# Split products of a compressed-interaction layer: which of their three matmul terms TensorE does on the first visit and which on the second

## The reference, cut to what matters

```python
def _cin(x, weights, biases):
    B, F, D = x.shape
    hidden = x
    finals = []
    for i, (w, b) in enumerate(zip(weights, biases)):
        size = w.shape[0]
        z = jnp.einsum('bhd,bfd->bhfd', hidden, x).reshape(B, hidden.shape[1] * F, D)
        y = jnp.einsum('bcd,oc->bod', z, w) + b[None, :, None]
        y = jax.nn.relu(y)
        if i != n_layers - 1:
            hidden, direct = (y[:, :size // 2, :], y[:, size // 2:, :])
        else:
            direct = y
        finals.append(direct)
    return jnp.concatenate(finals, axis=1).sum(-1)
```

## Time and profile before

| | us |
|---|---|
| median of 3 runs | 1091.94 (1091.52 to 1092.54) |
| the profiled execution, own time | 1092.62 |
| its span, first to last instruction | 1090.8 |
| TensorE busy | 1025.0 (94%) |
| VectorE busy | 944.4 (87%) |
| GpSimd busy | 915.5 (84%) |
| ScalarE busy | 734.9 (67%) |

### The profile page before, as it was taken

One profiled execution on the slowest core, in us unless ns is written; L12 is line 12 of the kernel. 1 busy time (PEld: TensorE's weight loads), 2 busy tenths in 40 slices (PEclk: granted clock), 3 DMA queues, 4 the chain that ended last, 5 costly groups with the idle time before them and its releaser, 6 DMA issues.

```text
span 1090.8 us, 10701 instructions
## 1 busy us (share of the span) xinstructions
PE 1025.0 (94%) x3493; PEld 651.4 (60%) x3493; DVE 944.4 (87%) x623; ACT 734.9 (67%) x907; POOL 915.5 (84%) x300
## 2 busy tenths in 40 slices
PE   2059999999999999999999999999999999999999
PEld 1025556656666666666666666666666666666664
DVE  4059999999999999999999999999998989888982
ACT  1036666767777677777777777777777777777761
POOL 7526878779999999999999899997989888988890
PEclk9569999999999999999999999999999999999999
DMA  4278777687878787778877878787777877786730
GB/s 137 55 188 200 194 186 184 180 198 190 210 178 205 183 213 187 192 191 199 207 185 192 201 181 208 182 206 194 194 184 194 204 183 187 191 208 184 183 84 1
DMA packets 142074, 196.89 MB, mean 180 GB/s; under 512 B 15858, under 2 KB 57458, under 8 KB 141891
## 3 DMA queue, kind: packets, MB, share of 16 engines
q1 hardware_dynamic: 137922, 192.01, 70.3%
q0 software_dynamic: 4096, 4.20, 1.8%
HBM read 175.18 MB, written 20.97 MB: 180 GB/s over the span
## 4 chain that ended last, share of the span: by engine, by line
PE 86%; DVE 4%; issue 4%; DMA 3%; ACT 2%; SPq 1%; DVEq 0%; ACTq 0%
PE py L610 40%; PE py L626 15%; PE py L616 14%; PE py L617 14%; DVE zf L498 2%; ACT zh L362 2%; PE py L631 1%; DMA xs<-x_dram 1%; DMA x_dram<-xf 1%; DMA xs<-in_L_rec_w 1%; PE pt L592 1%; DVE zl L515 1%; PE py L675 0%; PE pzS L675 0%; DVE zf L459 0%
## 5 line engine op out<-in xcount | busy, mean ns | idle before, releaser
L303 POOL TENSOR_TENSOR zl<-zf,zh 128x2048 fp32r<-128x2048 f32 x168 | 772.3, 4610 | 116.2 <-ACT zh L362 114.2
L498 DVE TENSOR_TENSOR zf<-xs,hid 128x2048 f32<-128x2048 f32 x256 | 583.3, 2283 | 67.1 <-ACT hid L377 51.9
L610 PE MATMUL py<-zf,wf 128*128 128x512 f32 x1072 | 485.2, 596 | 6.5 <-DVE zf L498 6.5
L362 ACT ACTIVATE zh<-zf 128x2048 fp32r<-128x2048 f32 x186 | 354.9, 1908 | 44.5 <-DVE zf L498 41.1
L610 PEld LDWEIGHTS py<-zf,wf 128*128 128x128 f32 x1072 | 203.5, 190 | 214.2 <-issue 194.2
L616 PE MATMUL py<-zh,wh 128*128 128x512 f32 x744 | 293.6, 395 | 8.7 <-ACT zh L362 8.7
L617 PE MATMUL py<-zh,wl 128*128 128x512 f32 x744 | 292.1, 393 | 0.0
L626 PE MATMUL py<-zl,wh 128*128 128x512 f32 x744 | 233.8, 436 | 0.0
L498 DVE TENSOR_TENSOR zf<-xs,px 128x2048 f32<-128x2048 f32 x64 | 146.4, 2288 | 37.8 <-DMA xs<-x_dram 35.9
L626 PEld LDWEIGHTS py<-zl,wh 128*128 128x128 f32 x744 | 135.9, 189 | 59.2 <-issue 29.2
L293 POOL DMA_INDIRECT emb<-in_tbl,idx x128 | 143.1, 1118 | 29.9 <-issue 24.5
(11 more groups left out here) (71 smaller groups left out, 439.8 us busy)
## 6 DMA issues: line engine op xcount, KB each, us to landing
xs<-x_dram SPq DMA_DIRECT2D x640, 256.0 KB
x_dram<-xf SPq DMA_DIRECT2D x64, 320.0 KB
emb<-in_tbl,idx POOLq DMA_INDIRECT x128
xs<-in_L_rec_w SPq DMA_DIRECT2D x2, 512.0 KB
xs<-in_L_rec_w SPq DMA_DIRECT2D x1, 1024.0 KB
wt<-in_W_top SPq DMA_DIRECT2D x1, 512.0 KB
wt1b<-in_W_top SPq DMA_DIRECT2D x1, 256.0 KB
wt1a<-in_W_top SPq DMA_DIRECT2D x1, 128.0 KB
```

The lines of the kernel that those rows point to most:

```text
L303: pool.tensor_tensor(zl[:, q], zf[:, s], zh[:, q].bitcast(F32), ALU.subtract).then_inc(lo["P"], 1)
L362: act.activation(zh[:, q], zf[:, s], ACT.Copy).then_inc(hi, 1)
L498: dve.tensor_tensor(zf[:, slot(u)], left, right, ALU.mult).then_inc(mult, 1)
L610: mm = pe.matmul(y, wf[:, w, h], zf[:, s, h], start=first and h == 0, stop=ends and h == T - 1)
```

## The change

Of a split unit's three terms, main now does wl x zh alone (4 matmuls) and late does the other two, wh x zl and wh x zh, in turn for each slab (8 matmuls). The order of the visits, the waits, the number of matmuls (12 for a unit) and everything on the other engines stay as they are. The "first" flag that clears the bank moves to wl x zh; the closing flag and the increment of used_split stay on the last matmul of late.

```diff
@@ -613,8 +613,7 @@
                     q, w = split_slot(u), SPLIT_NAMES.index(name)
                     pe.wait_ge(hi, NTH_SPLIT[u])
                     for h in range(T):
-                        pe.matmul(y, wh[:, w, h], zh[:, q, h], start=first and h == 0, stop=False)
-                        pe.matmul(y, wl[:, w, h], zh[:, q, h], start=False, stop=False)
+                        pe.matmul(y, wl[:, w, h], zh[:, q, h], start=first and h == 0, stop=False)
 
             def late(u):
                 name, g = u
@@ -623,7 +622,8 @@
                 q, w, y, ends = split_slot(u), SPLIT_NAMES.index(name), bank(u), closing(g) == u
                 need_low(pe, u)
                 for h in range(T):
-                    mm = pe.matmul(y, wh[:, w, h], zl[:, q, h], start=False, stop=ends and h == T - 1)
+                    pe.matmul(y, wh[:, w, h], zl[:, q, h], start=False, stop=False)
+                    mm = pe.matmul(y, wh[:, w, h], zh[:, q, h], start=False, stop=ends and h == T - 1)
                 mm.then_inc(used_split, 1)
```

## The result

The changed kernel takes 1111.6 us (median of five runs) against 1092.5 for the kernel before. The ratio of the two is 1.0165, 95% interval 1.0153 to 1.0178; of 1092.5 that makes 18.0 us (16.7 to 19.4), where the bare medians differ by 19.0. The kernel is slower, as forecast: 16.7 us and a time of 1108.6, in a range from 1099 to 1113, had been worked out.

What follows compares the result with a forecast made beforehand. TensorE, busy for 94% of the span, was taken to bound the kernel. Terms of 10.1 + 5.7 + 0.9 = 16.7 us on 1092.62 gave 1109.3, less 0.7 for the median 1108.6; range 1099 to 1113.

Steps and rivals of the forecast that it cites:

- The work is the same, only the moments move: Whole kernel: 744 matmuls of each term before and after; only the moments at which TensorE asks move.
- Part 1: Periods 0 to 10: each pair lasts 1.83 us longer; period 11 starts 11 steps of 0.915 us late, 10.1 us.
- Part 2: Periods 11 to 62: nine waits for D's product on VectorE at 0.62 us each, plus 0.1 us: 5.7 us.
- Periods 18 and 33: Two of eleven periods with low C on VectorE; older waits before A(19), A(34) absorb theirs: 0.1 us together.
- Late B: Periods 11 to 62: low part asked for a step earlier, B(26) tightest, 0.2 us short; nothing taken, 0.8 us if counted.
- the sign named against the prediction: Waits on zl appearing in the changed kernel would show the forecast wrong; no size given.
- Part 3: The end: closing late C(63) has 8 matmuls instead of 4 with nothing beside it: 0.9 us.
- A cheaper second load (1): In late, the pair's second load falls away, spacing 0.2145 us: 8 to 10.8 us less, 1098 to 1101; chance 0.08.
- a faster second matmul (2): In late, the second matmul follows at the load's 0.189 us: 30 us less, 1079; chance 0.03.
- Only the waits for D (3): Periods 0 to 10: if ScalarE absorbs the later turn_x, five steps go from the loss: 1104; chance 0.1.
- Nothing waits (4): Earlier needs are met because VectorE runs ahead once TensorE is late: 1092; chance 0.04.
- The clock (5): Odd periods' new 1.4 us waits drop TensorE to half clock; five falls of about 1.7 us give 1117; chance 0.05.

Runs made afterwards that it cites:

- e1: Changed kernel with main doing wh x zh and late wh x zl and wl x zh, same matmul numbers: 1111.3 us, ratio to kernel before 1.0174.
- e2: Kernel before with the change made for split units of periods 0 to 10 alone: 1103.5 us, ratio to kernel before 1.0102.
- e10: Changed kernel with turn_x ahead of main P in periods 1, 3, 5, 7 and 9 alone: 1100.8 us, ratio to kernel before 1.0066.
- e5: Kernel before with the change made for the C units alone: 1128.7 us, ratio to kernel before 1.0343.
- e3: Kernel before with the change made for split units of periods 11 to 42 alone: 1100.9 us, ratio to kernel before 1.0073.
- e4: Kernel before with the change made for split units of periods 43 to 63 alone: 1093.4 us, ratio to kernel before 1.0006.
- e9: Kernel before with the change made for the B units alone: 1111.4 us, ratio to kernel before 1.0164.
- e8: Kernel before with turn_x moved ahead of main P: 1087.5 us, ratio to kernel before 0.9956.

## Why the prediction was right, point by point

- **The work is the same, only the moments move.** Shown: equal counts, equal spacing, and e1 at the changed kernel's time.
- **Part 1, 10.1 us.** Shown. e2 gave 11.1 us for 11 steps and the boundary step, 11.0 expected; the loop's TensorE part grew by 1.84 us and its other part by 0.01; e10, which shortens only that loop, takes away 10.8 us. The waits before B that e5 shows have the same cause: high B stands behind xf in one queue.
- **Part 2, 5.7 us.** The mechanism held, the term was too small: the nine waits were priced at 0.62 us. From tail(12), the last before D(12), to tail(44) the changed kernel lost 18.1 - 11.1 = 7.0 us; e3 as a whole measured 8.0, with an interval of more than 2 us to either side. "0.30 us of slack" was the step that was off. In the traces TensorE never starts sooner than 0.05 us after the product's end, so only 0.25 of it was slack, and a unit that starts after a wait takes 3.70 us instead of 3.59, a cost of restart that rows 6 already had beside D(6) and that I had not counted: 0.915 - 0.25 + 0.11 = 0.78 us, times nine 7.0. Periods 18 and 33 were right: their waits were eaten by the older ones before A(19) and A(34), and they brought 0.1 us together.
- **Late B**, "I take nothing": wrong for two periods, and one reading was off. The tightest late B of the kernel before is not B(26) with 0.71 us but B(35) with 0.63; B(14) has 0.68 and B(20) 0.70. In the changed kernel two of them wait for their low part, B(20) and B(35). GpSimd's low B(20), then TensorE's late B(20):

```profile
418.25 4.65 POOL L303 TENSOR_TENSOR zl<-zf,zh 128x2048 fp32r<-128x2048 f32 x1
...
422.95 0.50 PE L625 MATMUL py<-zl,wh 128*128 128x512 f32 x1
```

  The low part ends at 422.90. The cover that the prediction counted on, the delay of TensorE from the V period before, was not there, as 18 and 33 had brought almost none. The tail starts move by 0.4 us at B(20) and by 0.5 at B(35), more than the 0.2 that the page counts as idle. It adds nothing to the sum: the D that follows, D(21) or D(36), then brings 0.4 or 0.3 us instead of 0.8. So the sign named against the prediction came; it touched the small terms only.
- **Part 3, 0.9 us.** From tail(60) to the end the difference goes from 18.1 to 19.0 us. e4's total cannot show it, since in it the first main A of the part is short as well and gives the same step back.
- **The sum** was 16.7 against 18.0 measured (16.7 to 19.4): 1.3 of it is part 2. The profiled execution itself stands 19.0 above the other, as it lost another 1 us at the start. The forecast time, 1108.6, is 3.0 below the measured one; besides part 2 and the difference between ratio and medians, the five runs of the kernel before had a median 0.6 us above that of the three it started from. By the prediction's own list the chances of slower are 0.93 and of faster 0.03, not 0.92 and 0.04.
- **Rivals.** A cheaper second load (1) and a faster second matmul (2): no, pairs are spaced like all others. Only the waits for D (3): no, it would leave 5 steps out, and e10 shows what the loop weighs. Nothing waits (4): no. The clock (5): no, it is 1.00 from 83 to 1100 us; the pauses of up to 1.4 us ahead of main B came and did not lower it. Before 83 us the two profiles do differ in clock, but not by the change (last section).

## What to carry to other kernels

When a hand-ordered engine is busy all the time, moving its work between two visits is not free though the sum stays: write down by how much each input is asked for sooner and each result handed on later, and set that against the slack read from the timeline. Do it for every wait of the engine and every loop through it: the two misses here (main A in e9, late B(20) and B(35)) were waits that had not been listed one by one. The sum over kinds of units is no guide (here A 0, B 18, C 37, all three 18 us); the loops are. A tiny instruction that another engine's queue stands behind, here a transpose ahead of xf and high B, deserves an earlier place before any of the large work is rearranged; here that alone made the kernel before 4.8 us faster.

## What the runs showed that was not expected

- A pause of TensorE costs more than its length: the eight f32 records of a whole unit that starts after one take 3.70 us from first start to last end instead of 3.59, and the first fp32r spacing is 0.31 us instead of 0.23, at a granted clock of 1.00.
- The start scatters between profiled executions, and in the two main profiles the difference is the clock. tail(1) stands between 0.8 us before (e1) and 2.5 us after (the changed kernel) that of the kernel before, in kernels that differ until then in A(0) or turn_x alone. Main P(1) and the window from 78 to 81 us (columns as rows 2) in the kernel before, then in the changed kernel:

```profile
77.82 3.60 PE L610 MATMUL py<-zf,wf 128*128 128x512 f32 x8
78.00:81.00 3.00, 3.00 (x9) 1.32 (x8) 2.94 (x3) 2.26 (x3) 2.55 (x3) 1.00 0.55 137
...
77.63 6.29 PE L610 MATMUL py<-zf,wf 128*128 128x512 f32 x8 [1.41 <-DVE zf L498]
78.00:81.00 3.00, 3.00 (x4) 1.11 (x4) 2.97 (x3) 2.11 (x4) 2.54 (x3) 0.50 0.30 99
```

  In both, the granted clock is at its lower level, 1.2 GHz, after the pause of 5.85 us before A(0); in the kernel before it is back at 2.4 GHz when P(1) runs, in the changed kernel it is not, and the unit takes 2.7 us longer. The new order is not needed for that: in e8, whose terms are dealt out as before, the same window has 0.50 too, and e1, with the changed numbers of matmuls, has 1.00.
- Loads are not saved when the stationary tile stays: in the changed kernel the two matmuls in a row with the same wh tile have two records of 0.19 us for their loads and the usual 0.23 us between them.
